# TensorE's order at the head of a unit: value products before the scores two units ahead, in an attention stage with one output bank

## What is computed

```python
x = x + 0.5 * _L0_ffn_ref(_layernorm(x), w_gate, w_up, w_down)
x = x + _L0_attn_ref(_layernorm(x), Wq, Wk, Wv, Wo, span_val)
x = x + 0.5 * _L0_ffn_ref(_layernorm(x), w_gate, w_up, w_down)
# in _L0_attn_ref: 16 heads of 64, causal
w = softmax(q @ k.T / DH + causal)
w = w * mask; w = w / (sum(w) + 1e-08)
out = (w @ v) @ Wo
```

## Time and profile before

| | |
|---|---|
| Median of 3 runs | 3317.49 us (3317.21 to 3319.31) |
| The profiled execution's own time | 3318.04 us |
| Its span in the profile | 3316.3 us |
| Busy: PE, PEld, DVE | 3150.5 us (95%), 2412.3 us (73%), 2717.3 us (82%) |
| Busy: ACT, POOL | 2460.8 us (74%), 1551.5 us (47%) |
| Granted TensorE clock, mean | 0.987 of full speed |

### The profile page before, as it was taken

One profiled execution on the slowest core, in us unless ns is written; L12 is line 12 of the kernel. 1 busy time (PEld: TensorE's weight loads), 2 busy tenths in 40 slices (PEclk: granted clock), 3 DMA queues, 4 the chain that ended last, 5 costly groups with the idle time before them and its releaser, 6 DMA issues.

```text
span 3316.3 us, 77709 instructions
## 1 busy us (share of the span) xinstructions
PE 3150.5 (95%) x28915; PEld 2412.3 (73%) x28915; DVE 2717.3 (82%) x5085; ACT 2460.8 (74%) x4837; POOL 1551.5 (47%) x1873
## 2 busy tenths in 40 slices
PE   4999997999999999999999999999999999799998
PEld 2677775777777777777777777777777777477776
DVE  7999995877877877787787778778777777799997
ACT  4787764777777777778777777777777777677775
POOL 3344432454455555455445545545545545333333
PEclk9999998999999999999999999999999999899999
DMA  3133313222322233222222223223222323111111
GB/s 112 39 93 87 115 40 89 52 59 67 91 57 70 65 84 72 67 78 66 60 81 74 68 65 82 70 53 96 72 55 52 100 58 102 32 52 58 58 58 39
DMA packets 160357, 231.36 MB, mean 70 GB/s; under 512 B 30064, under 2 KB 72176, under 8 KB 159984
## 3 DMA queue, kind: packets, MB, share of 16 engines
q1 hardware_dynamic: 159984, 226.38, 25.2%
HBM read 93.27 MB, written 32.38 MB: 38 GB/s over the span
## 4 chain that ended last, share of the span: by engine, by line
PE 69%; issue 6%; DVE 5%; ACT 2%; POOL 2%; DVEq 0%; ACTq 0%; POOLq 0%
PE at_t_ps L1500 14%; PE at_o_ps L1516 10%; PE at_side_ps L1414 10%; PE ffn_gu_ps L520 7%; PE at_s_ps L1489 6%; PE at_s_ps L1490 6%; PE at_side_ps L1467 4%; PE at_side_ps L1426 4%; PE ffn_down_ps L545 4%; DVE at_e_rows L1682 2%; PE at_side_ps L1455 2%; ACT at_eT_hi L1598 1%; PE ffn_hT_ps L485 1%; DVE at_eT_lo L1688 1%; DVE at_v_masked L1660 1%
## 5 line engine op out<-in xcount | busy, mean ns | idle before, releaser
L1688 DVE SCALAR_TENSOR_TENSOR at_eT_lo<-at_t_ps,at_eT_hi 128x512 f16<-128x512 f32 (+3 forms) x1536 | 853.2, 556 | 472.3 <-ACT at_eT_hi L1598 446.1
L1590 ACT ACTIVATE at_e_rows<-at_e_rows,at_neg_max 128x1024 f32<-128x1024 f32 (+7 forms) x1024 | 792.2, 774 | 214.1 <-DVE at_neg_max L1682 212.6
L1598 ACT ACTIVATE at_eT_hi<-at_t_ps 128x512 f16<-128x512 f32 (+3 forms) x1536 | 745.2, 485 | 191.3 <-PE at_t_ps L1500 182.4
L1682 DVE CUSTOM_DVE_ANT_0 at_e_rows<-at_s_ps,at_strip,keep_s_scale 128x1024 f32<-128x1024 f32 (+7 forms) x1024 | 828.0, 809 | 9.7 <-PE at_s_ps L1490 6.8
L1500 PE MATMUL at_t_ps<-at_ident,at_e_rows 128*128 128x128 f32 x4608 | 802.0, 285 | 0.1
L1516 PE MATMUL at_o_ps<-at_v_cols,at_eT_hi 128*128 128x132 f16 x4608 | 610.8, 221 | 11.0 <-ACT at_o_raw L1609 6.5
L1516 PE MATMUL at_o_ps<-at_v_cols,at_eT_lo 128*128 128x66 f16 x4608 | 568.2, 193 | 0.0
L1489 PE MATMUL at_s_ps<-at_kh_st,at_q_st 128*128 128x512 f16 (+3 forms) x1536 | 501.8, 327 | 17.9 <-DVE at_acc L1672 12.5
L1516 PEld LDWEIGHTS at_o_ps<-at_v_cols,at_eT_hi 128*128 128x128 f16 x4608 | 433.3, 97 | 91.4 <-DVE at_eT_lo L1688 23.9
L1500 PEld LDWEIGHTS at_t_ps<-at_ident,at_e_rows 128*128 128x128 f32 x4608 | 493.7, 141 | 3.9 <-issue 0.5
L1490 PE MATMUL at_s_ps<-at_kl_st,at_q_st 128*128 128x512 f16 (+3 forms) x1536 | 481.6, 327 | 0.0
(11 more groups left out here) (252 smaller groups left out, 6659.2 us busy)
## 6 DMA issues: line engine op xcount, KB each, us to landing
at_kh_st<-at_k_hi SPq DMA_DIRECT2D x256, 128.0 KB, 2.3
at_kl_st<-at_k_lo SPq DMA_DIRECT2D x256, 128.0 KB, 2.3
at_w_qk<-w_qk_split SPq DMA_DIRECT2D x65, 256.0 KB, 3.0
at_q_st<-at_q_hi SPq DMA_DIRECT2D x128, 128.0 KB, 2.4
at_q_st<-at_q_lo SPq DMA_DIRECT2D x128, 128.0 KB, 2.4
at_w_v<-w_v_split SPq DMA_DIRECT2D x66, 128.0 KB, 2.3
ffn_x_rows<-in_L_attn_query_dram SPq DMA_DIRECT2D x32, 256.0 KB, 3.2
ffn_x_res<-in_L_attn_query_dram SPq DMA_DIRECT2D x32, 256.0 KB, 3.8
```

What stands on the lines that cost most here:

```text
L1590: nc.scalar.activation(e_rows[:, n % 4, :w], e_rows[:, n % 4, :w], ACT.Exp, bias=neg_max[:, n % 4:n % 4 + 1], scale=-1.0).then_inc(sem("ex ...
L1598: nc.scalar.activation(eT[0][:, i % EBUF, :count * P], t_ps[i % TBUF][:, :count * P], ACT.Copy, scale=PSCALE).then_inc(sem("eT_hi"), 1)
L1682: nc.vector.tensor_tensor_reduce(e_rows[:, n % 4, :w], s_ps[n % 2][:, col:col + w], strip[:, SEQ - w:], keep["s_scale"][:, 0:1], BIGGEST, ...
L1688: nc.vector.scalar_tensor_tensor(out=eT[1][:, i % EBUF, :count * P], in0=t_ps[i % TBUF][:, :count * P], scalar=PSCALE, in1=eT[0][:, i % EB ...
```

## The change

In `pair_steps` the step *scores* of a unit's head is no longer put first, but behind the value products (and the copy) of the unit's first group, ahead of its transposes.

```diff
--- before.py
+++ after.py
@@ -656,8 +656,6 @@
     for n in range(NU):
         more = n + 2 < NU or after
         unit = ((n + 2) % NU, (n + 2) // NU)
-        if more:
-            steps.append(("scores",) + unit)
         for i in [i for i, (m, _, _) in enumerate(GROUPS) if m == n]:
             first = GROUPS[i][1] == 0
             if i >= LAG or before:
@@ -665,6 +663,8 @@
                 m = GROUPS[(i - LAG) % NG][0]
                 if LAST_GROUP[m] == (i - LAG) % NG:
                     steps.append(("copy", m, (i - LAG) // NG))
+            if first and more:
+                steps.append(("scores",) + unit)
             steps.append(("turn", i, 0))
             if i or before:
                 steps.append(("lo", (i - 1) % NG, (i - 1) // NG))
```

## The result

The changed kernel takes 3389.5 us (median of 4 runs, 3386.9 to 3390.3) against 3317.35 us of the kernel before (4 runs, 3316.2 to 3319.3). The ratio is 1.0215, with an interval of 1.0198 to 1.0233: slower by 72 us. The profiled execution took 3386.89 us, with a span of 3385.1.

A forecast was written before the change was run, and what follows sets the result against it. PE was taken to bound the kernel. Stalls of +135 us, -17 for transposes and -21 for the projection wait gave +97 on the profiled 3318.0, so 3415.0; the median of runs 3414.5, range 3350 to 3475.

The forecast's parts named there:

- What bounds the kernel: In attention PE is busy 391 of 400 us at full clock, so any moment it stands still is paid in full.
- The sites and what lowers them: Heads of even units, eight per pair: PE stalls for ACT's output copy, lessened where the copy starts earlier; +135 us.
- Transposes behind scores: At heads, transposes after scores rather than short value matmuls save up to 0.03 us each head; -17 us counted.
- A wait that ends elsewhere: Before the output projection, PE's existing wait is absorbed by the new stall at the fifth even unit; -21 us at best.
- The other moved parts: Later scores, transposes and exps in attention cost 0; other engines keep their lists and transfers, feed-forward is untouched.
- late scores: In attention, later scores delay DVE's max, then ACT's exps and copies: up to 90 us more, 3505; chance 0.05.
- the sign that I had set for being wrong: In attention, DVE waiting for scores would show the forecast wrong; no size given.
- The signs: In attention: fifth even unit waits longest, about 0.8 us; PE busy time hardly changes; projection wait nearly gone; clock 1.00.
- The first, a wait for `at_o_raw`: PE's list of waits would show the output copy at over 100 us, several hundred times; below 50 us meant wrong.
- ACT did not catch up: Rival: stalled PE lets ACT and DVE clear their backlog in attention, fewer stalls remain; +27 us, 3345; chance 0.08.
- The faster case: At even heads copies come early enough for no stalls, and PE gains from transposes; about 3280 us; chance 0.07.
- the drop of which the Trainium skill warns: Rival: PE's clock falls to 1.2 GHz for a twentieth of attention; +114 us, 3528; chance 0.03.

The follow-up runs named there:

- the run of even units alone: Against the kernel before, scores moved behind the first value products at the even heads only, odd heads unchanged: 3409.84 us against 3318.38, ratio 1.0280.
- The run of odd units alone: Against the kernel before, scores moved behind the first value products at the odd heads only, even heads unchanged: 3310.90 us against 3318.38, ratio 0.9978.
- the order with the cover kept: Against the kernel before, every head runs scores, first transposes, then value products: 3290.04 us against 3317.68, ratio 0.9914.
- The run that took out the fifth stall: Against the changed kernel, scores stay in front at the fifth even unit of each pair of heads: 3373.81 us, ratio 1.0170 to the kernel before.
- the kernel with transposes first: Against the kernel before, every head runs first transposes, then scores, then value products: 3312.79 us against 3317.68, ratio 0.9987.
- with two banks: Second output bank taken from the transposes (three to two): old order 3371.23 us, new order 3364.51, against 3318.38 for the kernel before.

## Why the prediction was right

It forecast 3414.5 us, 3350 to 3475, and slower by over 0.2% with 0.89; measured are 3389.5. Sign and mechanism hold; the size is 72 us for 97.

**What bounds the kernel.** Held. PE's busy time hardly moved, and its gaps grew by the 72 us that the kernel grew.

**The sites and what lowers them.** Held: 135 forecast, about 136 measured. By site it is less exact. New stall in us for a pair of heads, predicted as the mean of the two kinds of pair, measured as the mean of 62 pairs, without the wait that changed its place:

| site | 1 | 2 | 3 | 4 | 5 | 6 | 7 | 8 | sum |
|---|---|---|---|---|---|---|---|---|---|
| predicted | 0.30 | 0.11 | 0.26 | 0.32 | 0.65 | 0.08 | 0.40 | 0 | 2.12 |
| measured | 0.35 | 0.22 | 0.21 | 0.32 | 0.60 | 0.19 | 0.19 | 0 | 2.08 |

The seventh was half of what I took, with the reason that ACT is busy there until shortly before. It isn't: in the kernel before its copy starts 0.23 us after the start of the last odd value matmul in each of the 62 pairs, so it hangs on PE, and the small scores helped nearly as fully as at the eighth (0.49 us without them, in the run of even units alone). The second and sixth were twice the forecast. The good sum owes something to errors that cancel.

**Transposes behind scores.** Mis-sized: -17 taken, -29.3 measured, close to the full bound of -31. I had halved it with the reason that what is won before a stall only lengthens the stall. (Half of 31 is 15, not 17; the slip is worth 2 us of the sum.) The run of odd units alone shows a gain of 11 us in these gaps, but 7.5 in all; the order with the cover kept shows 26 in these gaps and 28 in all, which agree in part by chance, since there 12 us more stand before the first transposes and 10 less at the copy. Four transposes after scores, in the changed kernel:

```profile
1809.73 0.60 PE L1500 MATMUL at_t_ps<-at_ident,at_e_rows 128*128 128x128 f32 x4
1810.17 0.38 PE L1414 MATMUL at_side_ps<-at_xT_hi,at_w_qk 128*128 128x512 f16 x1
```

0.44 us to the next start, against 0.46 after value products. The Trainium skill (TensorE: Matmul & The Clock Gate, Step-by-step: what each phase is for) has PE pull the next weight load ahead of matmuls in flight. The trace agrees where scores stand ahead: the first transpose is followed after 0.109 us, the pace of transposes, or 0.115 behind scores of 128 columns. Behind the 66-column value matmuls it is followed only after 0.142 us (medians), so there the order does matter. That the weight load is the reason is not shown.

**A wait that ends elsewhere.** Held: -21 forecast, -16.5 measured. The run that took out the fifth stall confirms the tie: without it 12 us of this wait come back.

**The other moved parts.** Here is the part that failed most: I took 0 for all other waits of PE. They shrank by some 17 us (scores 7, value projection 6, first transposes of a group 4). As I read it, a PE that comes later finds more of its inputs ready; no run isolates that. So 97 + 1 (sites) - 12 (transposes) + 4 (projection) - 17 (other waits) = 73. I also took 0 for late scores. DVE waited 109.0 us for them, a hundred more than before, so the sign that I had set for being wrong did come; but the kernel with transposes first has 96.8 us of the same wait and is 5 us faster than before, and with two banks the change gains 7. As the cause of the loss this rival fell. How large its share within the 72 us is stays open.

**The signs.** Those for the longest site, PE's busy time, the projection and the clock came as written. The first, a wait for `at_o_raw` of over 100 us several hundred times, was wrong as a reading: the list shows 52.8 us, 159 times, near the 50 at which I had called myself wrong. The stalls are there, 170.5 us by starts, but the list hides short ones under modelled ends and gives 41.1 us to `eT_lo`.

**The rivals.** ACT did not catch up: that rival had the first, second, sixth and seventh site at 0, and they cost 0.35 + 0.22 + 0.19 + 0.19 = 0.95 us in a pair. The faster case did not come, and the clock stayed at its upper level beside gaps of 0.75 us on average at one site, and shorter ones at six more, in each pair of heads (some 36 us), so the drop of which the Trainium skill warns (same page, A second HAM failure mode: psum-queue depth-cycling) was not seen here.

## What to carry to other kernels

A short wait in the list of waits may mean that something covers it: before moving work, set the start of that work beside the end of what the next instruction needs, place by place. When a stall is added in front of a queue that has other waits behind it, part of it is paid out of those: here 17 + 17 of about 136 us, and removing one stall of 37 us gave 16. To gain from an order, keep the long work over the copy and move only what profits from its new neighbour.

## What was unexpected about the hardware

- The turnaround of a single output bank hardly varies: the copy takes 0.39 us, and the next matmul starts 0.143 to 0.146 us after its end at 365 of 371 stalled heads of the changed kernel and 68 of 71 of the kernel before.
- A transpose in float32 behind a 66-column matmul costs 0.142 us to the next start, behind scores 0.109 to 0.115. With the scores ahead of the first transposes of 1024 units, the transposes' busy time falls from 802.0 to 768.1 us.
- A PE that stalls at up to seven places in a pair of heads, some 36 us, kept a granted clock of 1.00 through attention (2354 us).
